# Local transformer: the one-token shift ahead of the MLP, from two products and a copy to transfers inside the on-chip memory

## The reference, cut to what matters

```
def shift_tokens(t):
    a, s = jnp.split(t, 2, -1)
    s = jnp.pad(s, ((0, 0), (1, 0), (0, 0)))[:, :-1]
    return jnp.concatenate([a, s], -1)

def ffn_layer(x, g, bln, W1, b1, W2, b2):
    mu = x.mean(-1, keepdims=True)
    var = ((x - mu) ** 2).mean(-1, keepdims=True)
    xn = (x - mu) / jnp.sqrt(var + 1e-05) * g + bln
    hg = xn @ W1 + b1
    a, gate = jnp.split(hg, 2, -1)
    return a * jax.nn.gelu(gate, approximate=False) @ W2 + b2
```

## Time and profile before

| | |
|---|---|
| median of 3 runs | 3143.26 us (3142.95 to 3143.5) |
| the profiled execution: its own time | 3143.12 us |
| its span in the trace | 3141.3 us |
| busy share: PE, DVE, ACT, POOL | 78%, 63%, 47%, 33% |
| the local transformer's loop, 695 to 2750 us | 2055 us |
| in it: PE, DVE, ACT, POOL busy | 1808, 1519, 1185, 881 us |

### The profile page before, as it was taken

The page is one execution under the profiler, slowest core; times in us unless marked ns, Lnnn a source line. Parts: engine busy times, 40 slices in busy tenths (PEclk is TensorE's granted clock), DMA queues, the critical chain, the costliest instruction groups (busy, mean ns, idle before and its releaser), DMA issues. The chain is left out here.

```text
span 3141.3 us, 71964 instructions
## 1 busy us (share of the span) xinstructions
PE 2442.7 (78%) x30424; PEld 1673.4 (53%) x30424; DVE 1963.5 (63%) x4358; ACT 1474.9 (47%) x2645; POOL 1031.8 (33%) x831
## 2 busy tenths in 40 slices
PE   6817758355889998998989898989898989758463
PEld 3515534233666666565656566656666666535252
DVE  4442235767887877777777868677868777234411
ACT  2303223423556566566656565656565656314120
POOL 0021220004544444444444434443444443000124
PEclk9958868658999999999999999999999999759676
DMA  7001100000101111102101110111100101020022
GB/s 259 3 18 51 34 15 1 0 1 24 29 25 28 53 29 32 29 15 59 29 25 29 53 36 25 28 53 29 32 15 25 35 25 29 15 82 2 9 64 57
DMA packets 71814, 110.10 MB, mean 35 GB/s; under 512 B 11394, under 2 KB 56712, under 8 KB 64966
## 3 DMA queue, kind: packets, MB, share of 16 engines
q1 hardware_dynamic: 67398, 97.88, 11.3%
q0 software_dynamic: 4096, 7.63, 0.8%
HBM read 42.29 MB, written 16.78 MB: 19 GB/s over the span
## 5 line engine op out<-in xcount | busy, mean ns | idle before, releaser
L2396 POOL TENSOR_TENSOR mem<-mem 128x512 f32<-128x512 f32 x384 | 468.0, 1228 | 938.4 <-DVE mem L2013 938.3
L2229 ACT ACTIVATE mem<-ps 128x512 f32<-128x512 f32 x384 | 216.5, 596 | 370.2 <-PE ps L1777 235.2
L1777 PE MATMUL ps<-mem 128*128 128x512 f32 x768 | 383.3, 622 | 4.3 <-DVE mem L2013 2.0
L2253 ACT ACTIVATE mem<-ps 64x512 f32<-64x512 f32 x384 | 228.7, 595 | 143.4 <-PE ps L1798 136.4
L2008 DVE TENSOR_TENSOR mem<-ps,mem 128x512 f32<-128x512 f32 x384 | 257.2, 670 | 22.9 <-ACT mem L2229 22.9
L2013 DVE TENSOR_TENSOR mem<-ps,mem 128x512 f32<-128x512 f32 x384 | 261.0, 680 | 0.0
L1786 PE MATMUL ps<-mem 128*128 128x512 f32 x384 | 208.6, 679 | 55.6 <-ACT mem L2239 55.6
L2020 DVE TENSOR_REDUCE mem<-mem 128x16 f32<-128x1024 f32 x192 | 232.4, 1210 | 0.0
L1848 PEld LDWEIGHTS ps<-mem 64*64 64x64 f32 x12288 | 190.7, 136 | 74.4 <-issue 73.0
L2403 POOL TENSOR_TENSOR mem<-mem 128x1024 f32<-128x1024 f32 x96 | 182.6, 1902 | 132.2 <-DVE mem L2055 132.2
L1814 PEld LDWEIGHTS ps<-mem 128*64 128x64 f32 x6144 | 194.7, 138 | 52.9 <-issue 52.9
(11 more groups left out here) (286 smaller groups left out, 4591.9 us busy)
## 6 DMA issues: line engine op xcount, KB each, us to landing
mem<-mem SPq DMA_DIRECT2D x48, 768.0 KB, 5.8
mem<-in_Wqkv SPq DMA_DIRECT2D x6, 1536.0 KB, 7.1
mem<-mem SPq DMA_DIRECT2D x36, 256.0 KB, 3.5
x<-mem SPq DMA_DIRECT2D x10, 512.0 KB, 6.5
mem<-x SPq DMA_DIRECT2D x16, 320.0 KB, 5.8
y<-mem SPq DMA_DIRECT2D x16, 320.0 KB, 2.5
mem<-in_W12T SPq DMA_DIRECT2D x8, 512.0 KB, 7.1
mem<-in_L3W SPq DMA_DIRECT2D x16, 256.0 KB, 5.4
```

Source lines behind the costliest of these rows:

```text
L1777: e.matmul(self.K.ps[:, o, :], self.columns(u, bb), self.K.l2[l % 2]["Wqkv"][:, 512 * i:512 * i + 512], start=True, stop=True, skip_group_ ...
L2229: e.activation(self.SQ[:, 512 * j:512 * j + 512], self.K.ps[:, (0, 1, 2, 5)[i], :], ACT.Square).then_inc(s("squared"), 1)
L2253: e.activation(self.Qbd[ur][q, bb, 4 * j:4 * j + 4, :, hp, :], pv[q], ACT.Copy).then_inc(s("placed"), 1)
L2396: e.tensor_tensor(t1[:, cols], t1[:, cols], self.T2[:, cols], ALU.add).then_inc(s("rotated"), 1)
```

## The change

The two products and ACT's copy go. In their place SP issues three transfers per half layer as soon as the attention has been added: one for rows 0 to 126 of all eight tiles to rows 1 to 127, and for each sequence one that takes row 127 of three tiles to row 0 of the tile behind. POOL sets row 0 of the first tile of each sequence to zero. The statistics wait for all three transfers and for both of POOL's instructions.

```
     def tensor / scalar (behind the loop)
-        self.pe_shift(e, f)
-        self.a_shift(e, f)
...
-    def pe_shift(self, e, f):
-        e.wait_ge(*s.at("attention_added", 4 * f + 4))
-        after(e, self.freed[7])
-        e.matmul(ps[:, 7, :], self.K.shiftm, X[:, c, 64:128], start=True, stop=False, skip_group_check=True)
-        e.matmul(o[:, :, 1:4, :], self.K.carrym, xs[:, :, 0:3, :], start=False, stop=True,
-                 skip_group_check=True).then_inc(s("shift_mm"), 1)
-        self.freed[7] = [s.at("mlp_shifted", f + 1)]
...
     def v_stats(self, e, f):
-        e.wait_ge(*s.at("mlp_shifted", f + 1))
-        e.wait_ge(*s.at("mlp_kept", f + 1))
+        e.wait_ge(*s.at("mlp_shifted", 48 * f + 48))
+        e.wait_ge(*s.at("mlp_kept", 2 * f + 2))
...
-    def a_shift(self, e, f):
-        if f >= 1:
-            e.wait_ge(*s.at("mlp_hidden", 6 * f))
-        e.wait_ge(*s.at("shift_mm", f + 1))
-        e.activation(self.K.XN[:, 0:8, 64:128], view(self.K.ps[:, 7, :], "p (t c) -> p t c", t=8), ACT.Copy
-                     ).then_inc(s("mlp_shifted"), 1)
...
     def p_kept(self, e, f):
         e.tensor_copy(K.XN[:, 0:8, 0:64], K.X[:, 8 * bp:8 * bp + 8, 0:64]).then_inc(s("mlp_kept"), 1)
+        first = view(K.XN[0:1, 0:8, 64:128], "p (b t) c -> p b t c", b=2)[:, :, 0, :]
+        e.memset(first, 0.0).then_inc(s("mlp_kept"), 1)
...
     def sync(self, e):
                 e.dma_start(self.VS[32:128], self.VN[u % 2][0:96]).then_inc(s("values_shifted"), 16)
+            if half == 0 and last and u % 4 == 0:
+                self.sync_shift(e, hl - 1)
...
+    def sync_shift(self, e, f):
+        s, X, XN, c = self.s, self.K.X, self.K.XN, slice(8 * (f % 2), 8 * (f % 2) + 8)
+        tiles = lambda z: view(z, "p (b t) c -> p b t c", b=2)
+        e.wait_ge(*s.at("attention_added", 4 * f + 4))
+        if f >= 1:
+            e.wait_ge(*s.at("mlp_hidden", 6 * f))
+        e.dma_start(XN[1:128, 0:8, 64:128], X[0:127, c, 64:128]).then_inc(s("mlp_shifted"), 16)
+        for b in range(2):
+            e.dma_start(tiles(XN[0:1, 0:8, 64:128])[:, b, 1:4], tiles(X[127:128, c, 64:128])[:, b, 0:3]
+                        ).then_inc(s("mlp_shifted"), 16)
```

More of the change, by code:

```diff
@@ L1627 @@
                   p_cols=NG, p_cols_too=NG, values_mm=4 * NU, values=4 * NU, values_shifted=16 * (2 * NU - NF),
-                  weighed=2 * NG, out_cols=2 * NG, projected=NU, attention_added=NU, shift_mm=NF, mlp_shifted=NF,
-                  mlp_kept=NF, mlp_rows=8 * NF, mlp_turned=2 * NF, mlp_cols=2 * NF, mlp_up=12 * NF, mlp_biased=12 * NF,
+                  weighed=2 * NG, out_cols=2 * NG, projected=NU, attention_added=NU, mlp_shifted=48 * NF,
+                  mlp_kept=2 * NF, mlp_rows=8 * NF, mlp_turned=2 * NF, mlp_cols=2 * NF, mlp_up=12 * NF, mlp_biased=12 * NF,
                   gelu=6 * NF, mlp_hidden=6 * NF, mlp_down=2 * NF, mlp_added=2 * NF, back=16, summed=1)
@@ L1748, in pe_beside @@
                 self.pe_turn_x(e, f, n, 7)
-            elif what == "shift":
-                self.pe_shift(e, f)
             elif what == "turn":
@@ L2293, in a_weighed @@
                          view(self.K.ps[:, 7 - wi, :], "p (b c q) -> p b c q", b=2, c=8), ACT.Copy).then_inc(s("out_cols"), 1)
-    def a_shift(self, e, f):
-        s = self.s
-        if f >= 1:
-            e.wait_ge(*s.at("mlp_hidden", 6 * f))
-        e.wait_ge(*s.at("shift_mm", f + 1))
-        e.activation(self.K.XN[:, 0:8, 64:128], view(self.K.ps[:, 7, :], "p (t c) -> p t c", t=8), ACT.Copy
-                     ).then_inc(s("mlp_shifted"), 1)
     def a_turn(self, e, f, bb):
```

## The result

The changed kernel took 3319.49 us (median of 4 runs, 3311.99 to 3323.38) against 3143.11 us before: a ratio of 1.056 (95% interval 1.0539 to 1.0581), 176 us slower. The forecast was 3350 us, with a range from 3285 to 3475.

A forecast was written before the change was run, and what follows sets the result against it. Chains of waits between PE and DVE, neither full, were taken to bound the kernel. New gaps of 260.4 us (158.0 plain, 102.4 behind loads) less 53.2 old give +207.2 on 3143.1: 3350 us, range 3285 to 3475.

The forecast's parts named there:

- The sign and the mechanism: At the shift, statistics wait for the transfer, so PE's and ACT's savings don't count: slower by 6.6%, chance 0.94.
- One engine: A single DMA engine carries all 1016 packets of the 127-partition transfer, 17.3 us; chance 0.87.
- The packet price: Each 256-byte packet of the long transfer costs 17 ns, with bounds of 13.4 and 26.8 ns.
- the fixed part and SP's wake-up: In each shift transfer, 2.35 us for everything but the packets, plus 0.1 us until SP wakes.
- the extra behind a load: At half layers 1, 3, 5 and 7, just behind a weight load, the gap is 25.6 us instead of 19.75.
- the small transfers add nothing: The two three-piece transfers, issued 0.57 us apart, lie behind the long one on the same engine and cost nothing.
- Queue order: Behind a weight load, the shift's packets start only when the load has passed, 7.1 us in at half layer 3.
- Carried to the end in full: The whole stall ahead of the statistics, +207.2 us over twelve half layers, reaches the kernel's end.
- The rival in which the loop gives 3.6 us a half layer back: PE's work ahead during the stall absorbs 40 us in all: 3310 us, chance 0.1.
- The clock: PE's clock falls after the new pause: zero to 2 us more a half layer, taken as zero, 20 us in the range.
- behind the weights: Long transfer spread over 16 engines or nearly, but waiting for the weight load: +13.3 us, 3156 us, chance 0.07.
- free: Transfer spread and not held up by the weight load: all twelve gaps 3.6 us, -10.0 us, 3133 us, chance 0.04.

The follow-up runs named there:

- 96 and 31: The changed kernel with the long 127-partition transfer cut in two, 96 and 31 partitions: 3208.54 us, ratio 1.0185 to the kernel before.
- the cut kernel: The changed kernel with the long 127-partition transfer cut in two, 112 and 15 partitions: 3165.99 us, ratio 1.0073 to the kernel before.
- The cut kernels: The changed kernel with the long transfer cut at 112 and 15 partitions, 3165.99 us; the same with the weight load moved behind the shift, 3148.61 us.

## Why the prediction was right

**The sign and the mechanism** held: DVE's next instruction waits for a transfer, PE's and ACT's savings are real (the 4.93 us of idle time went), and they don't count beside it.

**One engine** (chance 0.87) held, and is shown: a level 18 GB/s, gaps of 4.2 us with 112 and 15 partitions and 6.97 with 96 and 31, and the counts of packets. The lean I took from the row of 77 partitions was in the right direction, though that row alone would not have settled it.

**The packet price** is the term that was mis-sized: 17 ns taken, 14.1 ns measured. For 12 half layers of 1016 packets that is 12 x 1016 x 2.9 ns = 35.4 us, and 207.2 - 35.4 = 171.8 us, against 172.7 us measured in the gaps. The error is in the kind of number: I took how long a packet keeps its engine busy (26.8 ns from the earlier trace rows, 16.2 ns from the earlier trace rows) for the time from one packet to the next. As busy time 17 ns was close, since 18.1 ns is what the kernel after shows; but busy times overlap, and the transfer pays 14.1 ns a packet. The earlier trace rows could have told: 114.8% is more than all engines can be busy, and 16 x 2.00 us / 1372 = 23.3 ns from one 512-byte packet to the next. Half of that is 11.7 ns, so the lower bound of 13.4 was too high; that 14.1 lies above it was luck.

The other terms held: the fixed part and SP's wake-up come out at 2.7 to 2.85 us against 2.45; the extra behind a load at 5.5 us against 5.85. That the small transfers add nothing held too, but not as told: the second was not issued 0.57 us behind the first, since SP was held until 939.64 us (L2438 above). Still, the statistics started 1.57 us behind the end of that issue; in the cut kernel, where it is what comes last, they start 1.02 us behind it (1256.01 to 1257.03). So here the long transfer's own landing was later, by little.

**Queue order** held and is shown: behind the load the shift's packets began only when the load had nearly passed (1467 to 1469 us above), and with the load behind the shift the four long gaps became like the others, and the time fell from 3319 to 3289 us.

**Carried to the end in full** held. Against before the stage moved by +174.7 us for +172.7 in the gaps, +248.9 for +243.0, +144.6 for +150.9, +62.0 for +53.2, +19.0 for +24.1, -2.0 for -0.1, -20.9 for -16.7 and -39.0 for -39.4. Over gaps between 14 and 296 us the stage follows one for one, within 9 us. What makes these 9 us stays open. The rival in which the loop gives 3.6 us a half layer back (a figure for which no row was shown) is refuted: it would have missed by 40 us.

**The clock.** Windows of the kernel after, over the pause and behind it (busy time and count of PE, PEld, DVE, ACT and POOL; the last three numbers are the mean granted clock, the share of the DMA engines and GB/s):

```profile
930.00:940.00 10.00, 3.00 (x80) 1.65 (x72) 0.00 (x0) 0.00 (x0) 0.00 (x0) 0.77 0.09 20
940.00:950.00 10.00, 3.78 (x4) 1.12 (x4) 6.99 (x30) 2.33 (x5) 0.37 (x1) 0.55 0.00 1
```

The granted clock fell in the pause, as forecast: PE had stopped near 933 us, the mean of 0.77 and then of 0.55 means that 1.2 GHz was granted for 46% of the first stretch and 90% of the second, and 2.4 GHz for the rest. PE's first work behind the pause, L1783 at 944.98 us, took 3.78 us for four matmuls. The same four took half of that in the kernel before (L1786 there); the row is the next four, which took 3.78 us before and after (at 955.04 there). DVE's next long wait behind them, for ACT, is the second row here, from the kernel after:

```profile
938.40 1.88 PE L1786 MATMUL ps<-mem 128*128 128x512 f32 x4
963.64 0.19 DVE L2014 TENSOR_TENSOR mem<-mem 128x32 f32<-128x32 f32 x1 [3.92 <-ACT mem L2249]
```

From the start of the statistics to this place DVE took 963.64 - 941.21 = 22.43 us, and 953.22 - 930.68 = 22.54 us before. So PE's 1.9 us didn't reach DVE, and taking zero for the clock was right. The prediction's reading of the clock before was off, without effect on the sum: a mean of 0.66 between the levels 1 and 0.5 is two thirds of the stretch at 1.2 GHz, not half.

**The spread rivals.** The cut kernels come near them, though they have one issue more: 3156 us for "behind the weights", measured 3166; 3133 us for "free", measured 3149 with the load out of the way. The gaps explain most of it: 4.2 us and more where the rivals had 3.6, and 10.1 to 11.5 behind the load where they had 9.4, so that the twelve sum to 77.1 us and not 66.4, and to 52.8 and not 43.2.

## What to carry to other kernels

Before a copy goes to the DMA engines, look at its first dimension: 127 and 31 partitions ran on one engine, 96 and 112 on all, and the same 1016 packets took 14.3 us or some 1.6. Ask what the waiting engine does next: a transfer replaces idle time elsewhere only if it lands before that engine asks for it, and the queue ahead of it counts. And where an engine waits for a result that stands behind something it doesn't need yet, as the turned weights stood behind the shift, move it ahead first; here that gained 0.5% with two edited lines, when replacing the work in front of it by transfers, cut well, gained nothing.

## What was not expected of the hardware

SP doesn't come free when it has handed a transfer over. Behind the 1016 packets on one engine the issues of the two small transfers held SP for 14.60 us (L2438 above), for 19.9 to 20.3 us behind a weight load, and 1.47 us in the cut kernel. Nothing was late for it here, since SP's next copy comes some 30 us after it is free, but in a kernel that issues more from SP it could be.

Packets need not follow the shape that is written: eight rows of 512 bytes that touch were merged when the program was built and went as one packet of 4 KB. One engine moved 26.6 GB/s in them against 18 in packets of 256 bytes.
